# Three transposed layer norms done by chunk of 512 tokens, centred on TensorE, with routing or node products in between, in a two-layer graph and expert network

## What is computed

```python
x = x + gat_gru(layernorm(x), adj, ...)          # 3 attention heads over adj, then two GRU cells
x = x + ffn0(layernorm(x), ...)                  # 1 shared + 8 routed experts, D=128, F=512, top 2, gelu
x = x + bilinear(layernorm(x), adj, W1, W2, b)   # node = h@W1 (16), hw = h@W2 (16x128), relu(adj@sum(node*hw) + node@b)
x = x + ffn1(layernorm(x), ...)                  # 8 routed experts, F=256, top 2, relu
# layernorm(x) = (x - mean) / sqrt(var + 1e-5), over the 128 features
```

## Time and profile before

| | |
|---|---|
| median of 3 runs | 2110.42 us (2105.24 to 2110.78) |
| the profiled execution's own time | 2109.81 us |
| its span, first to last instruction | 2108.0 us |
| mean granted TensorE clock | 0.917 of full |
| busy share: PE, DVE, ACT, POOL | 87%, 78%, 63%, 10% |
| second norm and routing (A), PE | about 1120 to 1167 us |
| third norm and node products (B), PE | about 1568 to 1600 us |
| fourth norm and routing (C), PE | about 1879 to 1913 us |

### The profile page before, as it was taken

One profiled execution on the slowest core, in us unless ns is written; L12 is line 12 of the kernel. 1 busy time (PEld: TensorE's weight loads), 2 busy tenths in 40 slices (PEclk: granted clock), 3 DMA queues, 4 the chain that ended last, 5 costly groups with the idle time before them and its releaser, 6 DMA issues.

```text
span 2108.0 us, 28093 instructions
## 1 busy us (share of the span) xinstructions
PE 1825.0 (87%) x8989; PEld 880.6 (42%) x9138; DVE 1639.4 (78%) x1392; ACT 1336.2 (63%) x1427; POOL 208.0 (10%) x157
## 2 busy tenths in 40 slices
PE   2511964999999999999998899999998989997997
PEld 2511422444444444444446444444444334455443
DVE  7545267888988988989667587878767989866998
ACT  5765025877887788778434556565546877735875
POOL 0000200000000000100342000000005920000000
PEclk6555987999999999999997899999998999997999
DMA  8996045555446444554600211111002069922321
GB/s 353 407 429 221 1 172 193 153 157 180 137 152 182 145 150 149 170 158 151 222 12 0 83 50 40 50 40 50 10 21 120 0 246 428 420 101 83 110 99 70
DMA packets 70208, 311.78 MB, mean 148 GB/s; under 512 B 12918, under 2 KB 13398, under 8 KB 60262
## 3 DMA queue, kind: packets, MB, share of 16 engines
q1 hardware_dynamic: 70140, 310.88, 41.5%
HBM read 297.88 MB, written 12.98 MB: 147 GB/s over the span
## 4 chain that ended last, share of the span: by engine, by line
PE 51%; DVE 3%; ACT 2%; issue 2%; POOL 0%; ACTq 0%; DVEq 0%; POOLq 0%
PE psum L974 13%; PE psum L986 13%; PE psum L1059 8%; PE psum L923 8%; PE psum L1037 2%; PE psum L947 1%; PE psum L949 1%; PE psum L792 1%; DVE prod L1536 1%; PE psum L961 1%; PE psum L787 1%; PE psum L798 1%; PE psum L952 1%; PE psum L951 1%; ACT prod L740 1%
## 5 line engine op out<-in xcount | busy, mean ns | idle before, releaser
L620 ACT ACTIVATE ss<-KR,cls 128x1024 bf16<-128x1024 int16 x384 | 413.1, 1138 | 111.2 <-DVE pl L1373 110.5
L923 PE MATMUL psum<-ph,Tt 128*128 128x512 bf16 x1503 | 411.2, 380 | 8.3 <-DVE pl L1373 6.6
L696 ACT ACTIVATE hid<-psum,fB 128x1024 f32<-128x1024 f32 x208 | 227.1, 1112 | 184.3 <-PE psum L974 184.2
L974 PE MATMUL psum<-hTp,fW 128*128 (+1 forms) x1202 | 285.1, 383 | 11.7 <-ACT hid L696 3.7
L986 PE MATMUL psum<-hidp,fW 128*128 128x512 bf16 x1241 | 279.5, 379 | 2.3 <-DVEq L1502 1.9
L1370 DVE TENSOR_TENSOR ph<-ss,Ahi 128x3072 bf16<-128x3072 bf16 x128 | 228.3, 1784 | 58.6 <-PE psum L923 58.4
L1480 DVE TENSOR_TENSOR hidp<-hid,hidp 128x1024 bf16<-128x1024 f32 x208 | 245.4, 1221 | 26.6 <-ACT hidp L690 26.0
L923 PEld LDWEIGHTS psum<-ph,Tt 128*128 128x128 bf16 x1536 | 149.9, 98 | 190.3 <-issue 6.7
L1373 DVE TENSOR_TENSOR pl<-ss,Alo 128x3072 bf16<-128x3072 bf16 x128 | 227.2, 1775 | 0.0
L923 PE MATMUL psum<-pl,Tt 128*128 128x512 bf16 x753 | 226.0, 380 | 0.8
L974 PEld LDWEIGHTS psum<-hTp,fW 128*128 128x128 bf16 x1248 | 117.0, 98 | 168.9 <-ACT hid L696 32.0
(11 more groups left out here) (233 smaller groups left out, 2119.1 us busy)
## 6 DMA issues: line engine op xcount, KB each, us to landing
Ar<-in_adjT SPq DMA_DIRECT2D x32, 2048.0 KB, 13.2
Ab<-in_adjT SPq DMA_DIRECT2D x128, 512.0 KB, 4.1
A<-in_adjT SPq DMA_DIRECT2D x32, 2048.0 KB, 11.2
Tt<-T_d SPq DMA_DIRECT2D x128, 256.0 KB, 2.6
mB<-mk_d SPq DMA_DIRECT2D x64, 512.0 KB, 3.6
T_d<-tb SPq DMA_DIRECT2D x32, 256.0 KB, 2.0
RD<-rden_d SPq DMA_DIRECT2D x12, 512.0 KB, 6.0
fWs<-in_W SPq DMA_DIRECT2D x2, 2304.0 KB, 15.8
```

Of the source, the lines that this page charges most:

```text
L620: last = nc.scalar.activation(ss[s % 2][:, h, :], KR[:, h, rb * RB:(rb + 1) * RB], ACT.Sigmoid, scale=STEP, bias=cls[:, ds(t * HEADS + h, 1)])
L696: nc.scalar.activation(hid[j % HB][:, :], flat[:, j % 2 * CW:j % 2 * CW + CW], func, bias=fB1[:, j:j + 1]).then_inc(act_done[k], 1)
L923: last = nc.tensor.matmul(psum[:, 2 * h + q, :], Tt[s % AS][:, h, w, :], mv[:, q * CH:(q + 1) * CH], start=fresh and k == 0, stop=False, s ...
L974: last = nc.tensor.matmul(psum[:, j % 2 * 2 + b, :], fW[0][x][:, j * P:(j + 1) * P], hTp[y][:, ds(q * CW + b * CH, CH)], start=(w == 0), s ...
```

## The change

The norm is worked off in four pairs of chunks. `centre` (identity minus 1/128) is a new input, so that one matmul per chunk gives the centred values in PSUM (banks 0 to 2 in turn); ACT squares them and also copies them to `hT`; DVE scales `hT` in place by the spread root (banks 4 to 6 in turn). The variance goes to bank 7, routing or node products to bank 3. The order on PE is centre 0, 1; then for each pair b: variance of the pair, centring of pair b+1, routing or node products of pair b-1, spreading of pair b; and last the products of the last pair. `inverse_root` runs four times on 8 tiles. On DVE the low parts of pair b-1 stand between the eps step and `inverse_root` of pair b; on ACT the casts of pair b-1 stand behind the root of pair b.

The weights of the experts: for FFN 0 the cast and the low part of W1 move to POOL, into its stream of the GRU (a cast of 4608 columns after round 5, two subtractions of 2304 columns after rounds 9 and 13); the cast of W2 on ACT is made in two halves after chunks 4 and 5; its low part on DVE moves behind the choice of the experts (`low_weights` at the end of it), and PE waits for it before L999. For FFN 1 the casts on ACT are in halves after chunks 2 to 5, the low part of W1 follows chunk 4 on DVE, that of W2 also the choice of the experts. The low part of the large bilinear weight on POOL (L494) comes when its cast behind chunk 2 is done, in the midst of the norm.

```diff
+        centre = sb("centre", [P, P], F32, 200.75)
+            sp.dma_start(centre[:, :], a["centre"]).then_inc(g_in, 16)
...
 # POOL, in the GRU
+            half = FFN0[0] * FFN0[1] * P // 2
+            weighted_in(0, 3)
+            pool.wait_ge(r_in, 96)
+            pool.tensor_copy(fW[0][0][:, 0:2 * half], fWs[0][:, 0:2 * half]).then_inc(fw_hi, 1)
+            weighted_in(3, 5)
+            pool.wait_ge(fw_hi, 1)
+            pool.tensor_tensor(fW[0][1][:, 0:half], fWs[0][:, 0:half], fW[0][0][:, 0:half], ALU.subtract).then_inc(fw_lo, 1)
+            weighted_in(5, 7)
+            pool.tensor_tensor(fW[0][1][:, half:2 * half], fWs[0][:, half:2 * half], fW[0][0][:, half:2 * half],
+                               ALU.subtract).then_inc(fw_lo, 1)
+            weighted_in(7, NC)
...
             def bilinear_weights():
                 pool.wait_ge(b_hi, 1)
+                pool.tensor_tensor(bw1b[1][:, :], bw1[:, :], bw1b[0][:, :], ALU.subtract).then_inc(b_w_lo, 1)
+                pool.wait_ge(b_hi, 5)
                 pool.tensor_tensor(bw2[1][:, :], bw2f[:, :], bw2[0][:, :], ALU.subtract).then_inc(b_w_lo, 1)
-                pool.wait_ge(b_hi, 2)
-                pool.tensor_tensor(bw1b[1][:, :], bw1[:, :], bw1b[0][:, :], ALU.subtract).then_inc(b_w_lo, 1)
...
 # ACT
+        def lt_scalar(act, k, high):
+            def squared(q):
                 act.wait_ge(lt_centred, NC * k + q + 1)
                 if q >= 4:
                     act.wait_ge(lt_sum, NC * k + q - 3)
-                nc.scalar.activation(sqT[q % 4][:, :], hc[:, q * CH:(q + 1) * CH],
-                                     ACT.Square).then_inc(lt_squared, 1)
+                nc.scalar.activation(sqT[q % 4][:, :], psum[:, q % LNB, :], ACT.Square).then_inc(lt_squared, 1)
+                nc.scalar.activation(hT[:, q * CH:(q + 1) * CH], psum[:, q % LNB, :], ACT.Copy).then_inc(lt_copied, 1)
+
+            for b in range(NC // 2):
+                squared(2 * b)
+                squared(2 * b + 1)
+                act.wait_ge(ln_var, 3 + 4 * k + b)
+                nc.scalar.activation(stat[:, 3, 8 * b:8 * b + 8], stat[:, 2, 8 * b:8 * b + 8],
+                                     ACT.Sqrt).then_inc(ln_std, 1)
+                if b:
+                    high(2 * b - 2)
+                    high(2 * b - 1)
+            high(NC - 2)
+            high(NC - 1)
...
 # PE
+            def centred(q):
+                ready(q)
+                if q >= LNB:
+                    pe.wait_ge(lt_copied, NC * k + q - LNB + 1)
+                nc.tensor.matmul(psum[:, q % LNB, :], centre[:, :], xT[:, q * CH:(q + 1) * CH], start=True,
+                                 stop=True).then_inc(lt_centred, 1)
...
+            def spread(q):
+                pe.wait_ge(ln_normed, 3 + 4 * k + q // 2)
+                if q >= LNB:
+                    pe.wait_ge(ln_done, 2 + NC * k + q - LNB + 1)
+                for t in range(4 * q, 4 * q + 4):
+                    last = nc.tensor.transpose(psum[:, 4 + q % LNB, t % 4 * P:t % 4 * P + P],
+                                               stat[:, 4, t:t + 1].to_broadcast([P, P]), ident)
+                last.then_inc(ln_back, 1)
+
+            centred(0)
+            centred(1)
+            for b in range(NC // 2):
+                variance(2 * b)
+                variance(2 * b + 1)
+                if 2 * b + 2 < NC:
+                    centred(2 * b + 2)
+                    centred(2 * b + 3)
+                if b:
+                    rows(2 * b - 2)
+                    rows(2 * b - 1)
+                spread(2 * b)
+                spread(2 * b + 1)
+            rows(NC - 2)
+            rows(NC - 1)
...
             def ffn_tensor(k, nE, nF):
                 pe.sem_inc(down_done[k], hold)
-                pe.wait_ge(f_lo, (NC + 2) * (k + 1))
+                pe.wait_ge(f_lo, (NC + 1) * k + NC + k)
+                if k == 0:
+                    pe.wait_ge(fw_lo, 2)
...
                 pe.wait_ge(r_sel, 3 * k + 3)
+                pe.wait_ge(f_lo, (NC + 1) * k + NC + k + 1)
                 for t in range(NT):
...
 # DVE
+            def lt_vector(k, low):
+
+                def scaled(q):
                     dve.wait_ge(ln_back, 3 + NC * k + q)
-                    V.tensor_tensor(hT[:, xq], hc[:, xq], psum[:, q, :], ALU.mult).then_inc(ln_done, 1)
+                    dve.wait_ge(lt_copied, NC * k + q + 1)
+                    V.tensor_tensor(hT[:, q * CH:(q + 1) * CH], hT[:, q * CH:(q + 1) * CH], psum[:, 4 + q % LNB, :],
+                                    ALU.mult).then_inc(ln_done, 1)
+
+                for b in range(NC // 2):
+                    dve.wait_ge(lt_sum, NC * k + 2 * b + 2)
+                    V.tensor_scalar(stat[:, 2, 8 * b:8 * b + 8], psum[:, 7, 8 * b:8 * b + 8], EPS, None,
+                                    ALU.add).then_inc(ln_var, 1)
+                    if b:
+                        low(2 * b - 2)
+                        low(2 * b - 1)
+                    dve.wait_ge(ln_std, 3 + 4 * k + b)
+                    inverse_root(slice(8 * b, 8 * b + 8)).then_inc(ln_normed, 1)
+                    scaled(2 * b)
+                    scaled(2 * b + 1)
+                low(NC - 2)
+                low(NC - 1)
...
                 V.tensor_tensor(s1[:, :, :], s1[:, :, :], s2[:, :, :], ALU.add).then_inc(r_sel, 1)
-
+                low_weights(k, nE, nF, 1)
```

More of the change, by code:

```diff
@@ L278, in nlast @@
             return ds(q * CH, CH)
+        LNB = 3
         turn = [(t + NT // 2) % NT for t in range(NT)]
@@ L480, in _, with weighted_in @@
             pool.sem_inc(g_used, 2)
[L481 to L490, removed]
+            def weighted_in(lo, hi):
+                with pool.Fori(lo, hi) as q:
+                    for s in range(2):
+                        n = 2 * q + s
+                        pool.wait_ge(g_new, n + 3)
+                        pool.sem_inc(seen, 1)
+                        pool.tensor_tensor(gU[s][:, :], gU[s][:, :], dB[:, nlast(q)], ALU.mult).then_inc(g_scaled, 1)
+                        pool.wait_ge(g_scaled, n + 1)
+                        pool.wait_ge(g_used, n + 2)
+                        pool.sem_inc(seen, 1)
+                        pool.tensor_tensor(xT[:, nlast(q)], xT[:, nlast(q)], gU[s][:, :], ALU.add).then_inc(g_used, 1)
@@ L670, in _, with ffn_rows, weights, high @@
             candidate(2 * NC - 1, 1)
[L672 to L675, removed]
+            def ffn_rows(k, nE, nF):
+                half = nE * nF * P // 2
+                def weights(i, p):
+                    act.wait_ge(r_in, 96 * (k + 1))
+                    nc.scalar.activation(fW[i][0][:, p * half:(p + 1) * half], fWs[i][:, p * half:(p + 1) * half],
                                          ACT.Copy).then_inc(fw_hi, 1)
-            def ffn_scalar(k, nE, nF, func):
-                for q in range(NC):
+                def high(q):
                     act.wait_ge(ln_done, 3 + NC * 2 * k + q)
@@ L682, in ffn_scalar @@
                                          ACT.Copy).then_inc(fh_hi, 1)
+                    if k == 1 and q in (2, 3):
+                        weights(0, q - 2)
+                    if q in (4, 5):
+                        weights(1, q - 4)
+                return high
+            def ffn_scalar(k, nE, nF, func):
                 act.sem_inc(act_done[k], 2)
@@ L718, in ffn_scalar, with bilinear_rows @@
                     hidden(NW - 1, j)
-            ffn_weights(0, *FFN0)
-            lt_scalar(act, 0)
+            lt_scalar(act, 0, ffn_rows(0, *FFN0))
             ffn_scalar(0, *FFN0, ACT.Gelu)
[L723 to L727, removed]
-            for q in range(NC):
+            def bilinear_rows(q):
+                if q == 0:
+                    act.wait_ge(b_in, 64)
+                    nc.scalar.activation(bw1b[0][:, :], bw1[:, :], ACT.Copy).then_inc(b_hi, 1)
                 act.wait_ge(ln_done, 3 + NC + q)
@@ L731, in _ @@
                                      ACT.Copy).then_inc(b_hi, 1)
+                if q == 2:
+                    nc.scalar.activation(bw2[0][:, :], bw2f[:, :], ACT.Copy).then_inc(b_hi, 1)
+            lt_scalar(act, 1, bilinear_rows)
             act.wait_ge(b_node_ok, 1)
@@ L795, in lt_tensor @@
                 last.then_inc(lt_sum, 1)
-            pe.wait_ge(ln_normed, 3 + k)
-            for t in range(NT):
-                last = nc.tensor.transpose(flat[:, t * P:(t + 1) * P], stat[:, 4, t:t + 1].to_broadcast([P, P]),
-                                           ident)
-                if t % 4 == 3:
-                    last.then_inc(ln_back, 1)
+            def spread(q):
[21 more added lines that the diff above has]
+            rows(NC - 1)
         @block.tensor
@@ L1610 @@
         "consts": consts,
+        "centre": (np.eye(P) - 1 / P).astype(np.float32),
         "xT": g["x"].T,
```

141 lines of the change are left out of this document (67 added, 74 removed).

## The result

The changed kernel takes 2141.91 us (median of 4 runs, 2140.66 to 2143.33) where the kernel before took 2107.83 in the same session (2104.55 to 2110.78): 1.0162 times, 95% interval [1.0141, 1.0184]. It is slower, by 1.6%. The profiled execution took 2143.33 us, with a span of 2141.5 and a mean granted clock of 0.913 of full. Against that of before (2108.0) the span is 33.5 us longer; the sum had said 25.2.

The account below looks back on a forecast made before the run. PE, busy 87% of the span, was taken to bound the kernel, with only idle time to save. 2109.8 us plus A 7.2, B 8.4, C 2.4 and heads 7.2 gave 2135.0 us; range 2104 to 2146.

Parts of the forecast that it names:

- the sum: Total of the predicted losses: A 7.2, B 8.4, C 2.4 and heads 7.2 make 25.2 us.
- A: Second norm and routing, from the GRU's end to FFN 0: predicted end 1174 against 1166.75, +7.2 us.
- C: Fourth norm and routing before FFN 1: 32.5 us of work and 4 of waits, +2.4 us.
- B: Third norm and node products before the bilinear block: predicted end 1608.5 against 1600.1, +8.4 us.
- the rival with the lower clock throughout: Centring mixed with thin matmuls no longer raises PE's clock: A +11.5, B +12.5, C +7, total 2148 us; chance 0.15.
- GRU, POOL: POOL's long instructions in the GRU block DVE's updates: PE leaves 5.1 us later, DVE free at about 1140 for 1128.86.
- The rivals without a block: POOL does not hold up DVE in the GRU: 2117 us (chance 0.17), or 2101 if the overlap also pays (0.10).
- what remains at the middle of the clocks: 28 us: PE's work left in A after about 1140: spreading 5.1, variance 7.6, centring 5.1, routing 10.1, midway between higher and lower clock.
- the fall came within the variance matmuls in every stretch: Reading of the old profile that PE's clock dropped during the variance in A, B and C; used for taking middle clocks.
- the first rival: No block in the GRU: A -6.8 for +7.2, B without its block +4.4, total 2117 us; chance 0.17.
- Heads: Start of each FFN: W2's low part stands bare before the routing transposes, +4.95 and +2.28, together +7.2 us.
- The overlap pays: Pipeline starts undisturbed under the GRU's tail at the higher clock: A -12.3, total 2101 us; chance 0.10.

Follow-up runs that it names:

- e1_no_pool: Changed kernel with the cast and low part of FFN 0's W1 taken off POOL (cast on ACT, low part on DVE): 2129.32 us.
- e2_memset: Changed kernel with POOL's three long instructions in the GRU replaced by writes of a constant that read no SBUF: 2129.14 us.
- e3_gap: Changed kernel with W2's low part made on DVE ahead of its wait for the exponential of the choice: 2133.61 us.
- e12_fill_pipe: e8_first_only without the fourth norm's wait for all additions, plus ten products of zeros before each pair's spreading in A: 2103.18 us, 0.9981 of the kernel before.
- e5_old_pool: Kernel before, all three norms in old order, with only the three POOL instructions for FFN 0's W1 put into the GRU: 2128.44 us, ratio 1.0092.
- e8_first_only: Changed kernel with only the second norm by chunks, nothing long on POOL, W2's low part placed as in e3_gap: 2115.49 us, 1.0032 of the kernel before.

## Why the prediction was right

The time, 2141.9, lay in the range and on the likeliest side; the total was off by 7 us of 32. The kind of each loss was right, but that the sum came so near is in part luck: A was 6.1 us over its term and C 5.7, B 4.1 under, and 2.6 us came off ahead of the GRU, where nothing was changed. The total lies as near to the 2148 of the rival with the lower clock throughout as to the 2135.

- **GRU, POOL: right in kind and in size.** The rivals without a block are out. DVE was done 11.5 us later (11 forecast), PE left 7.1 later (5.1). PE's idle time in the GRU is 4.8 us, as forecast (5.1). The missing 2 us are busy time, 86.4 us for 84.1: two gate products behind the first wait took 1.12 us and behind the second 1.58 in the rows above, for 1.02 before, and the granted clock of the GRU was 0.963 for 0.981. That the port is held for a whole instruction, by an instruction that reads SBUF, is what the prediction took from the Trainium skill (SBUF — State Buffer, Who interferes with whom), and e1_no_pool and e2_memset bear it out: 0.68 us beside a write of 3.94, 4.44 beside a cast of 4.04.
- **A: +13.3 for +7.2.** The step that failed is "what remains at the middle of the clocks: 28 us". From DVE's last update to the end there were 39.6 us, 34 in the forecast: the waits were 5.0 (5.8 forecast), but the work took 34.6 for 28, at a mean granted clock of 0.54. The middle rested on a reading that is wrong for A: "the fall came within the variance matmuls in every stretch". In A before, the clock was down already in the last mean (2.04 us) and for all 64 variance records, 0.213 us each. The rival with the lower clock throughout had A's term (+11.5) nearly right; it was wrong in B.
- **B: +4.3 for +8.4.** The block came (4.13 us), in the last pair. B ran from 1584.7 to 1620.9; for its work I had taken the middle of the clocks, 30.2 us, and it was 25.7, since up to 1605 the granted clock was 0.98 (0.50 behind that). The waits were more than forecast, 10.5 us. The sum itself was slack: its terms as they stand, 30.2 and 1 + 3 + 2 + 2, end at 1606.5, not 1608.5, and without a block counted as 2 B is +6.4, not the +4.4 of the first rival. In other executions of the same B it was +5.7 to +6.4.
- **C: +8.1 for +2.4.** Nearly all of the miss is the clock: PE's idle time was 4.3 us (4 forecast), its work 37.8 (32.5). Half of the idle time was a wait that I had not seen, the 2.29 us of the first variance for all additions, by the bank it writes to; the waits I had named came out that much smaller. Five executions of other kernels with this same C took 37.5 to 37.7, this one 42.1; its third and fourth variance pairs took 2.82 and 3.41 us where the first two took 1.92 and 1.84. So 3.5 us belong to the order with its waits (3.0 of them idle time), and 4.6 to how the clock fell this time. No run takes the wait of 2.29 us alone out of the new order.
- **Heads: +8.5 for +7.2.** The low parts of 4.95 and 2.28 stand bare, as said; e3_gap gives 8.1 of it back. The 1.2 us over in FFN 1's head fit its up products at the lower clock, though no run separates them: ACT's second `hid` waited 1.45 us for PE (0.28 in e1_no_pool), and the exponential stands behind it.
- **The overlap pays (faster): right to be a rival, and out as the change stands.** Its condition was that the higher clock be kept; where e12_fill_pipe keeps it for 20 us, A gains 5.6 us, of the 12.3 worked out.

By the medians, then: 12.6 us are POOL's in the GRU (14 by the ratios on each chip), 8.3 the heads', and the rest, some 11 to 13, lies mostly in B and C, where it was read from single executions and by PE's idle time. Open is why in the same C the clock fell earlier in one execution than in five others, and in e5_old_pool's B; no run tells.

## What to carry to other kernels

Before work moves to an idle GpSimd, look at what VectorE does beside it: here each of three GpSimd instructions of 4 to 5 us that read SBUF held a two-input SBUF instruction of VectorE to its end, and the recurrence paid for it nearly in full. An overlap on TensorE is worth its saved waits only if the clock holds: here, in A with the blocks gone, it saved 2 us of waiting and lost as much to slower products, until the waits were filled with products of zeros. What was hidden for free (a weight split under a long matmul phase) has a price once it is moved behind the last wait of a chain; put it ahead of that wait.

## What was not expected of the hardware

- An idle TensorE of 0.57 us before the variance went with 4.8 us more in C in e8_first_only (1.4 in e5_old_pool), most of it behind the variance, as the granted clock of the same products was lower (0.62 for 0.80 in the routing). Taking the wait out gave it back.
- Ten products of zeros (1.25 us) ahead of each spreading held the granted clock at 1.00 for 20 us in which it was 0.74 and 0.61 without them; two ahead of each eight records of variance (a chunk) held it for only five chunks.
- Steps of DVE over eight columns (0.17 us) also wait for a whole GpSimd instruction: 1.15 us in e2_memset. Splitting one norm's `inverse_root` in four set them beside the GRU's tail. In the changed kernel one of those held reads a single SBUF tile (L1151, multiply and add constants), so two SBUF inputs are not the only case:

```profile
1139.50 1.26 POOL L493 TENSOR_TENSOR xT<-xT,gU 128x512 f32<-128x512 f32 x1 [0.20 <-POOL gU L489]
...
1139.55 1.24 DVE L1151 TENSOR_SCALAR stat<-stat 128x8 f32<-128x8 f32 x1
```

- DVE may get one instruction in first (1102.92, POOL's starts at 1103.03) and is held at the next. POOL's subtraction then shows 5.00 us, and 4.55 where DVE had not started before it (1127.36): it seems to wait for DVE's first, which no run tested.
